# A token-shift stage in one block with three groups under way, and squares and copies moved to ScalarE

## The chip, the core and the metric

The kernel runs on one core of one Trainium2 chip. The metric is the device time of one execution in microseconds (us). Engines are named as in the profile: PE is TensorE (matmuls, with PEld its weight loads), DVE is VectorE, ACT is ScalarE, POOL is GpSimd, SP issues the DMAs.

## What is computed

The program is a whole network over 32 sequences of 113 tokens (36 image patches and 77 text tokens) with 256 features: attention and experts, a state-space stage, a few more feed-forward stages, and at the end of it a token-shift stage and a product-key expert stage. The change touches the token-shift stage alone, whose reference, cut to what matters, is this (`_layernorm` is the outer norm without gain and bias, `_L3_attn_ref` the stage, and its result is added to the residual `h`):

```python
h = h + _L3_attn_ref(_layernorm(h, axis=-1), ...)
# in _L3_attn_ref, per sequence:
h = _layer_norm(x, ln1_g, ln1_b)
hp = _shift(h)
xk = h * mix_k + hp * (1.0 - mix_k)   # xv, xr alike
k = xk @ w_tk; v = xv @ w_tv; r = jax.nn.sigmoid(xr @ w_tr)
y = _wkv(time_decay, time_first, k, v)   # a scan over the tokens
x = x + r * y
h2 = _layer_norm(x, ln2_g, ln2_b)
ck = h2 * cmix_k + hp2 * (1.0 - cmix_k)   # cr alike, hp2 is h2 shifted
kk = jnp.square(jax.nn.relu(ck @ w_ck))
x = x + jax.nn.sigmoid(cr @ w_cr) * (kk @ w_cv)
```

`w_ck` is 256 x 1024 and `w_cv` 1024 x 256; all is fp32. `_wkv` keeps a running maximum, so that its exponentials don't overflow.

## The kernel before

The residual `h` stays in SBUF with the features on the partitions, as two blocks (DK = 2) of 128. Tokens go in 8 groups (GROUPS) of four sequences, 452 columns each (GT), which fill one PSUM bank. `rwkv` (L2184) first loads the weights in a block of its own, in which POOL clears five buffers (L2250 to L2254) and DVE prepares constants (L2259 to L2265). The weights of the channel part come on a semaphore `late`.

Then `step(front, back_cols)` (L2278) is called for group 0 alone, in a loop over seven pairs (the front of group g + 1 beside the back of group g), and for the back of group 7 alone. Each step is one block: all engines meet at its end, and `st.clear()` zeroes the stage's semaphores before the next.

The front of a group is: the input norm and the first norm (`Norm`, L87: mean on PE L107, centring on DVE L135, square on ACT L119 or L2392, variance on PE L113, Ln and Exp on ACT L124 and L127, scaling on DVE L142); gain and bias on DVE (L2484); for each of k, v and r a shifted copy on ACT (L2402), a mix on DVE (L2491) and eight matmul instructions (L2326); copies of k and v out of PSUM on ACT (L2414, L2417); the scan chain, which alternates DVE (L2505 to L2545) and ACT (Exp L2421, L2423, Ln L2426, Exp L2429, L2431); the sigmoids of r and of the gate on ACT (L2434, L2436, with a load of ACT's table ahead, and a load of the Exp/Ln table behind them at L2439); four DVE operations on both feature blocks (L2549 to L2556), which give `x2`; the second norm and its two mixes.

The back of a group is: the channel gate's eight matmul instructions (L2303), the raw copy of the gate on ACT (L2373) and its sigmoid (L2378), eight hidden blocks of four matmul instructions each (L2294), each with a Relu on ACT into one of two buffers (L2367) and its square on DVE (L2450), 32 matmul instructions of the output (L2314), and on DVE the add of `x2` to the residual (L2466), the product with the gate (L2459) and the last add (L2462).

Nothing is planned by a program: each engine's order is the order in the text of its function, and semaphores that count up to constants order the engines among each other.

Of the kernel before, what the change touches and what calls it, by code (L numbers as in the profile page):

```python
# [16 lines left out]
P = 128  # L17
# [67 lines left out]
class Norm:  # L85
# [2098 lines left out]
def rwkv(nc, h, c, wk, wv, wr, ck, cv, cr, cols):  # L2184

# [16 lines left out]
    with Stage(nc, "rw_late") as sl, Stage(nc, "rw") as st:  # L2202
# [11 lines left out]
        h1 = st.sbuf("h1", [P, DK, GT])  # L2214
        back = st.sbuf("back", [P, 5, DK, GT])
# [13 lines left out]
        x2 = st.sbuf("x2", [P, DK, GT])  # L2229
        relu = st.sbuf("relu", [P, 2, GT])  # L2230
# [4 lines left out]
                 "ev_done", "aa_done", "aap_done", "diff_done", "gate_done", "rg_done", "gd_done", "y_done", "ry_done", "x2_done", "h2_done",  # L2235
                 "c_mm", "relu_done", "sq_done", "cr_mm", "cg_raw", "cg_done", "cv_mm", "sk_done", "x3_done", "res_done")
        s = {x: st.sem(x) for x in names}
        with nc.Block() as block:
# [36 lines left out]
        def both(ap):  # L2275
            return ap.rearrange("p k (b n) -> p k b n", n=N)

        def step(front, back_cols):  # L2278

            with nc.Block(no_gpsimd_drain=True) as block:  # L2280
                @block.sync
                def _(sp):
                    if back_cols is None:
                        sp.wait_ge(late, 48)

                @block.tensor
                def _(pe):
                    def hidden(m):
                        if back_cols is None:
                            return  # L2290
                        if m >= 2:
                            pe.wait_ge(s["relu_done"], m - 1)
                        for k in range(DK):
                            mm = nc.tensor.matmul(ps[C_BANK[m % 2]][:, 0:GT], w_ck[:, k, m * P:(m + 1) * P], mixed[:, 3, k, :],  # L2294
                                                  start=(k == 0), stop=(k == DK - 1))
                        mm.then_inc(s["c_mm"], 1)

                    def channel_gate():
                        if back_cols is None:
                            return  # L2300
                        for m in range(DK):
                            for k in range(DK):
                                mm = nc.tensor.matmul(ps[O_BANK[m]][:, 0:GT], W["cr"][:, k, m * P:(m + 1) * P], mixed[:, 4, k, :],  # L2303
                                                      start=(k == 0), stop=(k == DK - 1))
                            mm.then_inc(s["cr_mm"], 1)

                    def channel_out():
                        if back_cols is None:
                            return
                        pe.wait_ge(s["cg_raw"], DK)  # L2310
                        for j in range(DK):
                            for m in range(HB):
                                pe.wait_ge(s["sq_done"], m + 1)
                                mm = nc.tensor.matmul(ps[O_BANK[j]][:, 0:GT], w_cv[:, m, j * P:(j + 1) * P], act2[:, m, :],  # L2314
                                                      start=(m == 0), stop=(m == HB - 1))
                            mm.then_inc(s["cv_mm"], 1)

                    def project(i, x, done):
                        pe.wait_ge(s["mix_done"], DK * (i + 1))
                        for m in range(DK):  # L2320
                            if i == 1 and m == 1:
                                pe.wait_ge(s["k_done"], 1)
                            if i == 2:
                                pe.wait_ge(*((s["k_done"], 2), (s["v_done"], 1))[m])
                            for k in range(DK):
                                mm = nc.tensor.matmul(ps[T_BANK[i][m]][:, 0:GT], W[x][:, k, m * P:(m + 1) * P],  # L2326
                                                      mixed[:, i, k, :], start=(k == 0), stop=(k == DK - 1))
                            mm.then_inc(done, 1)

                    if front is not None:  # L2330
# [783 lines left out]
```

## Time and profile before

| | us |
|---|---|
| three runs | 6014.45, 6021.89 (median), 6035.73 |
| the profiled execution, its own time | 6037.05 |
| its span | 6035.3 |
| PE, DVE, ACT, POOL busy in the span | 4920.7, 3587.9, 2192.0, 2261.7 |
| from the stage's first matmul to its last add | 621.4 |

A row of a table of stretches gives for each engine the time in which it works and the number of its instructions, then the granted clock of PE as a share of full speed. A row of a timeline gives the start, the time that the merged instructions take together, the engine, line and operation, what it writes and reads, how many there are, and in brackets how long the engine had been idle and who ended that. A matmul of the text on fp32 data is shown as two instructions.

### The profile page before, as it was taken

The numbers are of one execution on the slowest core, as the hardware profiler recorded it, in microseconds if no ns is written. First come the engines' busy times: TensorE is split into PE (matmuls) and PEld (weight loads), VectorE is DVE, ScalarE is ACT, GpSimd is POOL, SyncE is SP. The second block draws the span as 40 slices with busy tenths as digits, with TensorE's granted clock in tenths as the row PEclk, the third lists the DMA queues.
The fourth block names the chain that finished last, engine by engine and source line by source line (L and its number), as shares of the span: only waits on it lengthen the run. The fifth ranks groups of instructions, "written<-read, shape, count | busy, mean of one in ns | idle before, by whom it ended". The sixth has DMA issues, their size and how long they took to land. (4 is left out here: it accounts for less than half of the span.)

```text
span 6035.3 us, 64217 instructions
## 1 busy us (share of the span) xinstructions
PE 4920.7 (82%) x21148; PEld 3219.8 (53%) x21148; DVE 3587.9 (59%) x7080; ACT 2192.0 (36%) x4034; POOL 2261.7 (37%) x1366
## 2 busy tenths in 40 slices
PE   7988699368888878888688767857776999999999
PEld 4555377223333333333244437823335998989998
DVE  3664122269889889898742220055554876867776
ACT  3553011055555545656422232234441222222222
POOL 2442300469999989999700000000001212212211
PEclk8998899589999989899889878978887999999999
DMA  1003133212222222222200006600001000000000
GB/s 66 1 1 108 41 120 99 73 57 71 69 68 69 65 70 69 69 71 69 64 0 5 0 0 237 242 3 0 0 0 74 4 3 4 4 3 4 4 4 4
DMA packets 153762, 289.17 MB, mean 48 GB/s; under 512 B 24373, under 2 KB 135468, under 8 KB 144650
## 3 DMA queue, kind: packets, MB, share of 16 engines
q1 hardware_dynamic: 146426, 267.00, 13.6%
q0 software_dynamic: 6144, 14.04, 0.8%
q10 hardware_dynamic: 912, 4.63, 0.2%
q8 instruction: 147, 2.41, 0.2%
q14 instruction: 133, 1.09, 0.1%
HBM read 254.96 MB, written 33.42 MB: 48 GB/s over the span
## 5 line engine op out<-in xcount | busy, mean ns | idle before, releaser
L1496 PE MATMUL ssm_ps<-ssm_hc,net_ident 128*128 128x452 f32 x2048 | 957.1, 594 | 195.3 <-DVE ssm_hc L1729 111.0
L1659 POOL TENSOR_TENSOR ssm_dBu<-ssm_du,ssm_bc 128x904 f32<-128x904 f32 x512 | 1066.6, 2107 | 14.9 <-DMA ssm_bc<-ssm_rows 12.5
L1585 ACT ACTIVATE ssm_ps<-ssm_step,ssm_decay 128x448 f32<-128x448 f32 x1024 | 649.6, 638 | 665.6 <-DVE ssm_ps L1719 433.8
L1496 PEld LDWEIGHTS ssm_ps<-ssm_hc,net_ident 128*128 128x128 f32 x2048 | 390.4, 203 | 728.9 <-issue 343.1
L2925 POOL TENSOR_TENSOR peer_hot_cols<-peer_hot_cols,peer_codesT 128x512 f32<-128x512 f32 (+1 forms) x240 | 288.5, 1202 | 1159.2 <-DVE peer_hot_cols L2941 1159.2
L1719 DVE TENSOR_TENSOR_SCAN ssm_ps<-ssm_ps,ssm_dBu 128x452 f32<-128x452 f32 x512 | 565.2, 1104 | 128.1 <-ACT ssm_ps L1585 43.8
L1719 DVE TENSOR_TENSOR_SCAN ssm_hs<-ssm_ps,ssm_dBu 128x452 f32<-128x452 f32 x512 | 551.7, 1077 | 62.6 <-ACT ssm_ps L1585 35.8
L1668 POOL TENSOR_TENSOR ssm_hc<-ssm_hs,ssm_bc 128x904 f32<-128x904 f32 x256 | 539.5, 2107 | 74.8 <-DVE ssm_hs L1719 74.6
L2835 PE MATMUL peer_ps<-peer_xn,peer_down 128*128 128x226 f32 x2048 | 451.3, 366 | 24.2 <-issue 17.3
L2938 DVE TENSOR_TENSOR peer_hot_rows<-peer_ramp,peer_codesT 128x1024 f32<-128x1024 f32 (+1 forms) x240 | 284.5, 1186 | 280.0 <-PE peer_ps L2850 249.6
L2850 PEld LDWEIGHTS peer_ps<-peer_hot_cols,peer_hot_rows 128*128 128x128 f32 x3616 | 436.0, 192 | 23.8 <-DVE peer_hot_rows L2938 22.6
L2850 PE MATMUL peer_ps<-peer_hot_cols,peer_hot_rows 128*128 128x64 f32 x3616 | 427.7, 272 | 18.7 <-DVE peer_hot_rows L2938 18.7
L2835 PEld LDWEIGHTS peer_ps<-peer_xn,peer_down 128*128 128x128 f32 x2048 | 381.9, 195 | 30.6 <-issue 25.6
L2877 PE MATMUL peer_ps<-peer_hid,peer_up 128*128 128x226 f32 x2048 | 396.7, 354 | 1.5 <-DVE peer_hid L2957 1.5
L2877 PEld LDWEIGHTS peer_ps<-peer_hid,peer_up 128*128 128x128 f32 x2048 | 387.6, 189 | 6.1 <-issue 1.8
L1729 DVE TENSOR_TENSOR ssm_hc<-ssm_ps,ssm_bc 128x452 f32<-128x452 f32 x512 | 309.0, 603 | 0.0
L2904 ACT ACTIVATE peer_hid<-peer_ps 128x452 f32<-128x452 f32 x256 | 140.3, 548 | 416.4 <-PE peer_ps L2835 416.4
L2897 ACT ACTIVATE peer_weight<-peer_ps 128x512 f32<-128x512 f32 (+1 forms) x240 | 144.5, 610 | 287.1 <-PE peer_ps L2850 287.1
L2622 POOL IOTA peer_ramp<- 128x128 f32 x1 | 0.2, 238 | 632.1 <-ACTq L2611 632.1
L2250 POOL MEMSET rw_back<- 128x4520 f32 x1 | 3.9, 3865 | 598.2 <-POOLq L73 598.2
L1283 POOL DMA_INDIRECT sh_got<-slots_out,moe_from_slot x64 | 64.7, 1011 | 420.6 <-SPq L1274 393.1
L1542 PE MATMUL ssm_ps<-ssm_ln_out,ssm_w_in 128*128 128x452 f32 x256 | 138.7, 673 | 97.0 <-DVE ssm_conv L1738 96.8
(422 smaller groups left out, 8304.1 us busy)
## 6 DMA issues: line engine op xcount, KB each, us to landing
ssm_bc<-ssm_rows SPq DMA_DIRECT2D x256, 452.0 KB, 3.6
ex_w<-in_l_ffn_w SPq DMA_DIRECT2D x66, 1024.0 KB, 9.4
moe_w_gu<-in_moe_gate_up SPq DMA_DIRECT2D x16, 704.0 KB
slots_in<-rt_zeros SPq DMA_DIRECT2D x17, 640.0 KB, 8.5
moe_rows_in<-slots_in SPq DMA_DIRECT2D x16, 512.0 KB
slots_out<-xp_rows_out SPq DMA_DIRECT2D x16, 512.0 KB
moe_w_dn<-in_moe_down SPq DMA_DIRECT2D x16, 384.0 KB
peer_down<-in_peer_down_t SPq DMA_DIRECT2D x1, 4096.0 KB, 16.4
```

Source lines behind the costliest of these rows:

```text
L1496: nc.tensor.matmul(Y_BANK[j][:, 0:GT], c["ident"][:, :], hc[:, q % 2, j, :], start=False, stop=(n == S - 1))\
L1585: nc.scalar.activation(rows(dA(i % 2))[:, :, lo:lo + N - 1], rows(step[hf.d][:, j, :])[:, :, lo:lo + N - 1], ACT.Exp, scale=decay[hf.d][:, ...
L1659: nc.gpsimd.tensor_tensor(dBu[:, q % 2, j:j + 2, :], du[hf.d][:, j:j + 2, :], bc[:, q % RING, 0:1, :].to_broadcast([P, 2, GT]), ALU.mult). ...
L1668: nc.gpsimd.tensor_tensor(hc[:, q % 2, 0:2, :], hs[:, q % 2, :, :], bc[:, q % RING, 1:2, :].to_broadcast([P, 2, GT]), ALU.mult).then_inc(s ...
L1719: nc.vector.tensor_tensor_scan(flow(state, hf.d), flow(dA(i % 2), hf.d), flow(dBu[:, q % 2, j, :], hf.d), 0.0, ALU.mult, ALU.add).then_inc ...
L1729: nc.vector.tensor_tensor(hc[:, q % 2, j, :], HS_BANK[:, 0:GT], bc[:, q % RING, 1, :], ALU.mult)\
L2835: mm = nc.tensor.matmul(ps[1 + i % 3][:, jj * PT:(jj + 1) * PT], down[:, m, i * J + jj, :], xn[:, m, :], start=(m == 0), stop=(m == DK - 1))
L2850: mm = nc.tensor.matmul(ps[4 + ch % HB][:, t * PB * EB:(t + 1) * PB * EB], hot_rows[:, at % HB, t, :], hot_cols[:, at % HB, t, :], start=T ...
L2877: mm = nc.tensor.matmul(ps[5 + m][:, 0:PT], w_up[:, j, m * P:(m + 1) * P], hid[:, j, :], start=(j == 0), stop=(j == EB - 1))
L2897: nc.scalar.activation(weight[:, :, :, t0:t0 + n], ps[4 + ch % HB][:, 0:n * PB * EB].rearrange("p (t b j) -> p j b t", b=PB, j=EB), ACT.Co ...
L2925: nc.gpsimd.tensor_tensor(hot_cols[:, at % HB, 0:n, :], hot_cols[:, at % HB, 0:n, :], codesT[:, 2, t0:t0 + n].unsqueeze(2).to_broadcast([P ...
L2938: nc.vector.tensor_tensor(hot_rows[:, at % HB, 0:n, :], ramp[:, :].unsqueeze(1).to_broadcast([P, n, P]), codesT[:, 0, t0:t0 + n].unsqueeze ...
```

## The change

The stage becomes one block. On PE and ACT ten iterations, on DVE eleven, each hold work of three groups: the norms and projections of group i (`early`), the scan chain and second norm of group i - 1 (`mid`), and the channel part of group i - 2 (`late_`). Every wait counts over all groups. `kp`, `v` and `x` get a second buffer; k, v and r share the banks 2 and 3, and the second norm gets bank 1. The square of the Relu goes from DVE to ACT and is made in place; the copy into `AAp` goes from DVE to ACT; the channel gate's sigmoid reads PSUM directly, without the raw copy. `x2` lives in `d1`. The functions that only got a group index (`squares`, `shifted`, `decays`, `weights`, `mix`, `output`, `sums`, `lags`, `averages`, `differences`, `mixed_rows`) issue the operations of before.

```diff
...
-    def __init__(self, st, mean_ps, var_ps, name="ln", width=GT):
+    def __init__(self, st, mean_ps, var_ps, name="ln", width=GT, square=None, out=None):
...
-        self.square = st.sbuf(f"{name}_square", [P, DK, width])
+        self.square = square or st.sbuf(f"{name}_square", [P, DK, width])
...
-        self.out = st.sbuf(f"{name}_out", [P, DK, width])
+        self.out = out or st.sbuf(f"{name}_out", [P, DK, width])
...
-        norms = [Norm(st, ps[0], ps[0], f"ln{i}") for i in range(3)]
-        T_BANK = ((1, 2), (3, 1), (2, 3))
-        C_BANK, O_BANK = (4, 5), (6, 7)
+        T_BANK, C_BANK, O_BANK = (2, 3), (4, 5), (6, 7)
+        x = st.sbuf("x", [P, 2, DK, GT])
+        norms = [Norm(st, ps[0], ps[0], "ln0", out=x)]
+        norms.append(Norm(st, ps[0], ps[0], "ln1", square=norms[0].square))
+        norms.append(Norm(st, ps[1], ps[1], "ln2"))
...
-        kp = st.sbuf("kp", [P, DK, GB, N + 1])
-        v = st.sbuf("v", [P, DK, GT])
+        kp = st.sbuf("kp", [P, 2, DK, GB, N + 1])
+        v = st.sbuf("v", [P, 2, DK, GT])
...
-        x2 = st.sbuf("x2", [P, DK, GT])
-        relu = st.sbuf("relu", [P, 2, GT])
...
-                nc.gpsimd.memset(kp[:, :, :, :], 0.0)
+                nc.gpsimd.memset(kp[:, :, :, :, :], 0.0)
...
+                def project(g, i, x, done):
+                    pe.wait_ge(s["mix_done"], DK * (3 * g + i + 1))
+                    for m in range(DK):
+                        if i == 0 and g:
+                            pe.wait_ge(s["rg_done"], DK * (g - 1) + m + 1)
+                        elif i:
+                            pe.wait_ge((s["k_done"], s["v_done"])[i - 1], DK * g + m + 1)
...
+                def hidden(g, m):
+                    pe.wait_ge(s["mix2_done"], 2 * DK * g + DK)
+                    if HB * g + m >= 2:
+                        pe.wait_ge(s["relu_done"], HB * g + m - 1)
...
+                def channel_gate(g):
+                    pe.wait_ge(s["mix2_done"], 2 * DK * (g + 1))
+                    if g:
+                        pe.wait_ge(s["sk_done"], DK * g)
...
+                def channel_out(g, j):
+                    pe.wait_ge(s["cg_done"], DK * g + j + 1)
+                    for m in range(HB):
+                        pe.wait_ge(s["sq_done"], HB * g + m + 1)
...
+                for i in range(GROUPS + 2):
+                    early, mid, late_ = i, i - 1, i - 2
+                    if i == 2:
+                        pe.wait_ge(late, 48)
+                    if live(early):
+                        if early:
+                            pe.wait_ge(norms[1].log_ready, early)
+                        norms[0].tensor_mean(nc, pe, c["ones"], lambda k: h[:, k, group_cols(early)])
+                    if live(mid):
+                        project(mid, 2, "wr", s["r_mm"])
+                    if live(late_):
+                        hidden(late_, 0)
+                        hidden(late_, 1)
+                    if live(early):
+                        norms[0].tensor_var(nc, pe, c["ones"], early + 1)
+                    if live(late_):
+                        channel_gate(late_)
+                        hidden(late_, 2)
+                        hidden(late_, 3)
+                    if live(early):
+                        pe.wait_ge(norms[0].ready, early + 1)
+                        norms[1].tensor_mean(nc, pe, c["ones"], lambda k: x[:, early % 2, k, :])
+                    if live(late_):
+                        hidden(late_, 4)
+                        hidden(late_, 5)
+                    if live(early):
+                        norms[1].tensor_var(nc, pe, c["ones"], early + 1)
+                    if live(late_):
+                        hidden(late_, 6)
+                        hidden(late_, 7)
+                        channel_out(late_, 0)
+                    if live(early):
+                        project(early, 0, "wk", s["k_mm"])
+                    if live(mid):
+                        pe.wait_ge(s["x2_done"], mid + 1)
+                        if mid:
+                            pe.wait_ge(norms[2].log_ready, mid)
+                        norms[2].tensor_mean(nc, pe, c["ones"], lambda k: d1[:, k, :])
+                    if live(early):
+                        project(early, 1, "wv", s["v_mm"])
+                    if live(mid):
+                        norms[2].tensor_var(nc, pe, c["ones"], mid + 1)
+                    if live(late_):
+                        channel_out(late_, 1)
...
+                def rectify(g, m):
+                    at = HB * g + m
+                    act.wait_ge(s["c_mm"], at + 1)
+                    if g:
+                        act.wait_ge(s["cv_mm"], DK * g)
+                    nc.scalar.activation(act2[:, m, :], ps[C_BANK[m % 2]][:, 0:GT], ACT.Relu).then_inc(s["relu_done"], 1)
+                def square(g, m):
+                    act.wait_ge(s["relu_done"], HB * g + m + 1)
+                    nc.scalar.activation(act2[:, m, :], act2[:, m, :], ACT.Square).then_inc(s["sq_done"], 1)
+                def channel(g, m):
+                    if live(g):
+                        for n in (m, m + 1):
+                            rectify(g, n)
+                        for n in (m, m + 1):
+                            square(g, n)
...
+                def gates(g):
+
+                    if g:
+                        act.wait_ge(s["gd_done"], g)
+                        act.wait_ge(s["ry_done"], g)
...
+                for i in range(GROUPS + 2):
+                    early, mid, late_ = i, i - 1, i - 2
+                    if live(early):
+                        squares(0, early)
+                    if live(mid):
+                        decays(mid, 0)
+                        decays(mid, 1)
+                    channel(late_, 0)
+                    if live(early):
+                        norms[0].scalar_root(nc, act, c["eps"], early + 1)
+                    if live(mid):
+                        for k in range(DK):
+                            act.wait_ge(s["s_done"], DK * mid + k + 1)
+                            if mid:
+                                act.wait_ge(s["aap_done"], DK * mid)
+                            nc.scalar.activation(aa[:, k, :], s_[:, k, :], ACT.Ln).then_inc(s["ln_done"], 1)
+                    channel(late_, 2)
+                    if live(mid):
+                        weights(mid, 0)
+                    if live(early):
+                        squares(1, early)
+                    if live(mid):
+                        weights(mid, 1)
+                        gates(mid)
+                    if live(late_):
+                        channel_gate(late_)
                     nc.scalar.preload_act_table_set(EXP_LN)
+                    if live(early):
+                        norms[1].scalar_root(nc, act, c["eps"], early + 1)
+                    channel(late_, 4)
+                    if live(mid):
                         for k in range(DK):
+                            act.wait_ge(s["aa_done"], DK * mid + k + 1)
+                            if mid:
+                                act.wait_ge(s["diff_done"], DK * mid)
+                            nc.scalar.activation(AAp[:, k, :, 1:N + 1], rows(aa[:, k, :]), ACT.Copy).then_inc(s["aap_done"], 1)
+                    channel(late_, 6)
+                    if live(early):
+                        shifted(early, 0)
+                        shifted(early, 1)
+                    if live(mid):
+                        squares(2, mid)
+                    if live(early):
+                        shifted(early, 2)
                         for k in range(DK):
+                            act.wait_ge(s["k_mm"], DK * early + k + 1)
+                            if early >= 2:
+                                act.wait_ge(s["dl_done"], DK * (early - 1))
+                            nc.scalar.activation(kp[:, early % 2, k, :, 1:N + 1], rows(ps[T_BANK[k]][:, 0:GT]), ACT.Copy)\
+                                .then_inc(s["k_done"], 1)
+                    if live(mid):
+                        norms[2].scalar_root(nc, act, c["eps"], mid + 1)
+                    if live(early):
                         for k in range(DK):
+                            act.wait_ge(s["v_mm"], DK * early + k + 1)
+                            if early >= 2:
+                                act.wait_ge(s["y_done"], early - 1)
+                            nc.scalar.activation(v[:, early % 2, k, :], ps[T_BANK[k]][:, 0:GT], ACT.Copy).then_inc(s["v_done"], 1)
+                    if live(mid):
+                        shifted_channel(mid, 3)
+                        shifted_channel(mid, 4)
...
+                def exponents(g, k):
+                    dve.wait_ge(s["M_done"], DK * g + k + 1)
+                    if g:
+                        dve.wait_ge(s["x3_done"], g)
+                        dve.wait_ge(norms[2].centred_ready, g)
+                        dve.wait_ge(s["aa_done"], DK * g)
...
+                for i in range(GROUPS + 3):
+                    early, mid, late_ = i, i - 1, i - 2
+                    if live(mid):
+                        maxima(mid, 0)
+                        maxima(mid, 1)
+                    if live(early):
+                        centre(0, early, h[:, :, group_cols(early)])
+                    if live(mid):
+                        exponents(mid, 0)
+                        exponents(mid, 1)
+                    if live(late_ - 1):
+                        output(late_ - 1, 1)
+                    if live(mid):
+                        sums(mid, 0)
+                        sums(mid, 1)
+                    if live(early):
+                        input_scale(early)
+                    if live(mid):
+                        lags(mid, 0)
+                        lags(mid, 1)
+                    if live(early):
+                        dve.wait_ge(norms[0].ready, early + 1)
+                        centre(1, early, x[:, early % 2, :, :])
+                    if live(mid):
+                        averages(mid, 0)
+                        averages(mid, 1)
+                    if live(early):
+                        if early:
+                            dve.wait_ge(s["h1_done"], DK * early)
+                        norms[1].vector_scale(nc, dve, early + 1)
+                        scaled(early, norms[1], h1, G1, B1, s["h1_done"], s["mix_done"], DK * 3 * early)
+                    if live(mid):
+                        differences(mid, 0)
+                        differences(mid, 1)
+                    if live(early):
+                        mix(early, 0)
+                    if live(mid):
+                        mixed_rows(mid)
+                    if live(early):
+                        mix(early, 1)
+                    if live(mid):
+                        dve.wait_ge(s["x2_done"], mid + 1)
+                        cols = group_cols(mid)
+                        nc.vector.tensor_tensor(h[:, :, cols], d1[:, :, :], h[:, :, cols], ALU.add).then_inc(s["x3_done"], 1)
+                        centre(2, mid, d1[:, :, :])
+                    if live(late_):
+                        output(late_, 0)
+                    if live(early):
+                        mix(early, 2)
+                    if live(mid):
+                        if mid:
+                            dve.wait_ge(s["h2_done"], DK * mid)
+                        norms[2].vector_scale(nc, dve, mid + 1)
+                        scaled(mid, norms[2], h2, G2, B2, s["h2_done"], s["mix2_done"], 2 * DK * mid)
+                        mix_channel(mid, 3)
+                        mix_channel(mid, 4)
...
-            st.clear()
-        step(group_cols(0), None)
-        with nc.Fori(0, GROUPS - 1) as g:
-            step(group_cols(g + 1), group_cols(g))
-        step(None, group_cols(GROUPS - 1))
+        st.clear()
         sl.clear()
```

## Rows read from the trace of the kernel before

**Rows 1.** The page's head.
```profile
span 6035.3 us, 64217 instructions
```
**Rows 2.** Stretches: first step, a middle step, the last, all (us, then PE, PEld, DVE, ACT, POOL, PEclk, DMA).
```profile
3925.60:3995.20 69.60, 29.28 (x48) 11.48 (x48) 34.37 (x48) 25.65 (x40) 0.00 (x0) 0.67 0.00 0
...
4214.90:4290.00 75.10, 52.71 (x120) 24.76 (x120) 41.92 (x61) 31.42 (x51) 0.00 (x0) 0.82 0.00 0
...
4515.10:4547.00 31.90, 29.97 (x72) 14.64 (x72) 8.65 (x13) 7.73 (x12) 0.00 (x0) 0.92 0.00 1
3925.60:4547.00 621.40, 422.67 (x960) 197.31 (x960) 336.55 (x488) 253.31 (x409) 0.00 (x0) 0.82 0.00 0
```
**Rows 3.** Timeline of PE in the middle step and the last.
```profile
4215.29 3.38 PE L107 MATMUL rw_ps<-net_h,net_ones 128*128 x4 [14.16 <-PEq L73]
...
4239.07 2.18 PE L2294 MATMUL rw_ps<-rw_mixed,rw_ck 128*128 128x452 f32 x4 [3.07 <-ACT rw_relu L2367]
4241.04 4.54 PE L2326 MATMUL rw_ps<-rw_mixed,rw_wk 128*128 128x452 f32 x8
...
4253.00 12.30 PE L2314 MATMUL rw_ps<-rw_act,rw_cv 128*128 128x452 f32 x32
4268.18 3.19 PE L107 MATMUL rw_ps<-rw_x,net_ones 128*128 128x452 f32 x4 [2.88 <-DVE rw_x L2556]
4273.61 2.59 PE L113 MATMUL rw_ps<-rw_ln_square,net_ones 128*128 128x452 f32 x4 [2.25 <-ACT rw_ln_square L119]
...
4520.87 12.30 PE L2294 MATMUL rw_ps<-rw_mixed,rw_ck 128*128 128x452 f32 x32
```
**Rows 4.** Timeline of DVE at the border between two steps.
```profile
4290.18 1.10 DVE L2466 TENSOR_TENSOR net_h<-rw_x,net_h 128x904 f32 x1 [4.88 <-PEq L73]
```
**Rows 5.** Groups of DVE instructions in the stage (busy us, mean ns, idle before).
```profile
L2450 DVE TENSOR_TENSOR rw_act<-rw_relu 128x452 f32<-128x452 f32 x64 | 39.5, 627 | 43.8 <-ACT rw_relu L2367 43.8
...
L2541 DVE COPY rw_AAp<-rw_aa 128x452 f32<-128x452 f32 x14 | 4.7, 380 | 0.0
```
**Rows 6.** Groups of ACT instructions in the stage.
```profile
L2402 ACT ACTIVATE rw_back<-rw_h,rw_rest 128x448 f32<-128x448 f32 x70 | 42.2, 660 | 53.4 <-DVE rw_h L2484 53.4
...
L2367 ACT ACTIVATE rw_relu<-rw_ps 128x452 f32<-128x452 f32 x64 | 34.5, 540 | 45.8 <-PE rw_ps L2294 45.8
...
L119 ACT ACTIVATE rw_ln_square<-rw_ln_centred 128x904 f32<-128x904 f32 x14 | 13.4, 959 | 77.0 <-DVE rw_ln_centred L135 77.0
L124 ACT ACTIVATE rw_ln_log_var<-rw_ps,net_eps 128x452 f32<-128x452 f32 x21 | 13.4, 638 | 47.1 <-PE rw_ps L113 47.1
...
L2436 ACT ACTIVATE rw_gate<-rw_s,rw_first_neg 128x452 f32<-128x452 f32 x14 | 8.7, 673 | 0.0
...
L2423 ACT ACTIVATE rw_d<-rw_d 128x452 f32<-128x452 f32 x14 | 8.1, 582 | 0.2
```
**Rows 7.** Timeline: a hand-off from DVE to ACT, and a table load on ACT.
```profile
4218.83 1.10 DVE L135 TENSOR_TENSOR rw_ln_centred<-net_h,rw_ps 128x904 f32<-128x904 f32 x1 [2.62 <-PE rw_ps L107]
...
4219.96 0.96 ACT L119 ACTIVATE rw_ln_square<-rw_ln_centred 128x904 f32<-128x904 f32 x1 [3.73 <-DVE rw_ln_centred L135]
...
4259.39 1.28 ACT L2434 ACT_TABLE_LOAD   x1
4260.69 0.99 ACT L2434 ACTIVATE rw_rg<-rw_ps 128x452 f32<-128x452 f32 x2
```
**Rows 8.** Timeline of PE in the first step.
```profile
3925.67 3.35 PE L107 MATMUL rw_ps<-net_h,net_ones 128*128 128x452 f32 x4 [14.63 <-PEq L73]
...
3948.99 5.58 PE L2326 MATMUL rw_ps<-rw_mixed,rw_wk 128*128 128x452 f32 x8 [5.55 <-DVE rw_mixed L2491]
...
3957.43 2.82 PE L2326 MATMUL rw_ps<-rw_mixed,rw_wr 128*128 128x452 f32 x7
```
**Rows 9.** Timeline of the setup, POOL and DVE.
```profile
3916.71 0.86 POOL L2251 MEMSET rw_kp<- 128x912 f32 x1
...
3920.04 0.82 DVE L2263 TENSOR_SCALAR rw_drift<-rw_drift,rw_cols 128x452 f32<-128x452 f32 x2 [0.83 <-POOL rw_drift L2254]
```

More of the change, by code:

```diff
@@ L2273, in rows, with flat @@
             return ap.rearrange("p (b n) -> p b n", n=N)
[L2275 to L2292, printed above, removed]
+        def flat(ap):
+            return ap.rearrange("p b n -> p (b n)")
@@ new lines, in live, with _, mean @@
+        def live(g):
+            return 0 <= g < GROUPS
+        with nc.Block(no_gpsimd_drain=True) as block:
+            @block.tensor
+            def _(pe):
+                def mean(j, g, ap):
+                    norms[j].tensor_mean(nc, pe, c["ones"], ap)
+                def project(g, i, x, done):
[5 more added lines that the diff above has]
+                            pe.wait_ge((s["k_done"], s["v_done"])[i - 1], DK * g + m + 1)
@@ L2293, in hidden @@
                         for k in range(DK):
-                            mm = nc.tensor.matmul(ps[C_BANK[m % 2]][:, 0:GT], w_ck[:, k, m * P:(m + 1) * P], mixed[:, 3, k, :],
+                            mm = nc.tensor.matmul(ps[T_BANK[m]][:, 0:GT], W[x][:, k, m * P:(m + 1) * P], mixed[:, i, k, :],
                                                   start=(k == 0), stop=(k == DK - 1))
[L2296 to L2328, printed above, removed]
@@ new lines, in channel_gate @@
+                def channel_gate(g):
+                    pe.wait_ge(s["mix2_done"], 2 * DK * (g + 1))
+                    if g:
+                        pe.wait_ge(s["sk_done"], DK * g)
+                    for m in range(DK):
+                        for k in range(DK):
+                            mm = nc.tensor.matmul(ps[O_BANK[m]][:, 0:GT], W["cr"][:, k, m * P:(m + 1) * P], mixed[:, 4, k, :],
+                                                  start=(k == 0), stop=(k == DK - 1))
+                        mm.then_inc(s["cr_mm"], 1)
@@ new lines, in _, with squares, shifted @@
+            @block.scalar
+            def _(act):
+                def rectify(g, m):
[13 more added lines that the diff above has]
+                            square(g, n)
+                def squares(j, g):
+                    act.wait_ge(norms[j].centred_ready, g + 1)
+                    if j == 0 and g:
+                        act.wait_ge(norms[1].var_ready, g)
+                    nc.scalar.activation(norms[j].square[:, :, :], norms[j].centred[:, :, :], ACT.Square)\
+                        .then_inc(norms[j].square_ready, 1)
+                def shifted(g, i):
+                    act.wait_ge(s["h1_done"], DK * (g + 1))
@@ L2432, in _, with decays @@
-                    for k in range(DK):
-                        act.wait_ge(s["r_mm"], k + 1)
-                        nc.scalar.activation(rg[:, k, :], ps[T_BANK[2][k]][:, 0:GT], ACT.Sigmoid).then_inc(s["rg_done"], 1)
+                        nc.scalar.activation(rows(back[:, i, k, :])[:, :, 1:N], rows(h2[:, k, :])[:, :, 0:N - 1],
+                                             ACT.Copy, scale=rest[:, MIXES[i], k:k + 1]).then_inc(s["back2_done"], 1)
+                def decays(g, k):
+                    act.wait_ge(s["d1_done"], DK * g + k + 1)
+                    nc.scalar.activation(d1[:, k, :], d1[:, k, :], ACT.Exp).then_inc(s["a_done"], 1)
+                    act.wait_ge(s["d2_done"], DK * g + k + 1)
+                    nc.scalar.activation(d2[:, k, :], d2[:, k, :], ACT.Exp).then_inc(s["a_done"], 1)
```

338 lines of the change are left out of this document (131 added, 207 removed).

## The prediction

> **What bounds the kernel now.** I read the page first: 6035.3 us of span, and a program in stages, so what counts is the stage that the diff touches [rows 1]. The table of stretches comes second, with its borders laid on the first and last instruction of the stage's steps [rows 2]. Between the setup and the last residual add lie 621.4 us: a first step of 69.6 us, seven steps of 72 to 75 us (the row of 75.1 stands for them), and a last one of 31.9 us. In a step of 75.1 us PE is busy 52.7 us, DVE 41.9, ACT 31.4. No engine is full: the step is a chain through all three, with PE the longest.
>
> PE's own need comes from two rows of 32 matmuls in 12.30 us [rows 3]: about 0.378 us each, at a granted clock of full speed, for 120 matmuls 45.4 us a group. The other 7.3 us of PE's 52.7 are the half clock: after a wait of 14.16 us four matmuls take 3.38 us instead of about 1.7, and after one of 3.07 us eight take 4.54 instead of 3.2. The step's granted clock is 0.82. The rest of the step, 75.1 less 52.7, is PE waiting.
>
> The timeline of one step says where [rows 4]. The next step's first vector instruction begins at 4290.18 after 4.88 us without work: in this time all engines stand at the block's end and start. Before that PE is idle from 4276.2 on, 14 us with the border, since the second norm, its shift and its mixes run on DVE and ACT alone. PE's two other stops are 3.07 us (a Relu on ACT) and 2.9 plus 2.25 us (the second norm) [rows 3].
>
> **The change, part by part.** (1) Nine blocks become one. The borders go: eight of some 4.9 us, 39 us, and nothing takes their place, since nothing has to be zeroed between groups. (2) In one iteration PE now gets matmuls of three groups, so the norms and mixes of one are covered by the channel matmuls of another. The price is the depth: ten iterations on PE and ACT for eight groups, where there were nine steps. (3) The square of the Relu and the AAp copy go from DVE to ACT. DVE loses 8 x 0.627 and 2 x 0.38 [rows 5], 5.8 us a group, and goes from 41.9 to 36.1. ACT has no row of a 452-wide Square; Exp of that width, 0.58, bounds it from above, and the 904-wide Square (0.96) less half the 904 columns' time from below, about 0.49 [rows 6]. Eight of them, overlapping like the other ACT instructions, add 4 to 5 us. With the copies of AAp in, and the raw copies of the gate out, ACT has some 35 us a group. Neither engine is the bound of an iteration that PE needs 45.4 us for; they count where PE waits on them.
>
> So I walk the new order around once, in the rows' durations. A hand-off costs 0.03 us between DVE and ACT (centred ends at 4219.93, its square begins at 4219.96) [rows 7], and about 0.2 us behind PE's last matmul. Instructions of one engine that don't depend on each other overlap by 0.09 us or so. PE stops at two places of an iteration.
>
> First stop, the hidden product 6, which waits for the Relu 4. That Relu stands in ACT's order behind the first norm's second half. From the end of mean 1: 0.2 + centre 1.13 + square 0.87 + two Exp 0.96 + table load 1.30 + two gates 1.14 + four sigmoids 1.80 + table load 1.30 + log 0.67 + exp 0.48 + Relu 0.58 = 10.4 us. PE covers 12 matmuls of it (4.5 us) and waits 5.9.
>
> Second stop, the v projection, which needs the bank that the copy of k empties, and that copy stands on ACT behind the square of the second norm and a shift. From the end of mean 2: 0.2 + centre 1.13 + square 0.87 + two shifts 1.14 + copy 0.58 = 3.9 us, all of it wait.
>
> The circle closes through PE: the other 108 matmuls are 40.8 us, and 40.8 + 10.4 + 3.9 = **55.2 us** at full clock. To this comes the half clock. Today a step's stops cost 7.3 us of it, 1.3 to 2.4 us for each [rows 2, 3]. Two stops of 5.9 and 3.9 us I set at 2 us each: **59.3 us**. Bounds: nothing, 55.2; or both stops' following eight matmuls at half speed and one more stretch, 66.
>
> What is ahead and behind this: iteration 0 has one group only and the same instructions as today's first step, from its first matmul at 3925.67 to the last projection's place at 3957.43 [rows 8]: 31.8 us. Iteration 1 has 48 matmuls (18.1 us) and waits of 2.6 (input norm) and 3.0 us (first norm), as today's 2 to 3, of 8.1 before the k projection (today's 5.55 of the first step [rows 8] and the two table loads now ahead of the root), and of 4 us (the copy of k). Its clock I take from the first step, 0.67 [rows 2]: two thirds of the matmuls at half speed, 12 us. That is 48. Iterations 2 to 7 are 6 x 59.3 = 356, plus 6 us in the first of them, where the channel products wait for mixes that were late in iteration 1. Iteration 8 has 88 matmuls (33.3) and two waits. Before the hidden product 6: 0.2 + Relu 0.45 + two squares 0.96 + four Exp 1.92 + load 1.30 + gates and sigmoids 2.94 + load 1.30 + Relu 0.58 = 9.65, less the 3.0 of the products 4 and 5, 6.6; before the second norm's variance today's 2.3 [rows 3]; with 1 us of clock 43. The last has 72 (27.2), the same chain without Exps and gates (5.7 less 3.0 = 2.7), 1.6 of clock and 1.3 of output: 33. Sum: 31.8 + 48 + 362 + 43 + 33 = **518 us** for what are 621.4 now: 103 less. Some 44 of the 518 are half clock (4.1 in each of six iterations, 2 in the first, 12 and the rest in the fill and the end). The setup grows by one memset of 0.86 us on POOL ahead of the one that DVE already waits 0.83 us for [rows 9]: 0.8 back. The gain is 102.6 us.
>
> Edits at nothing: the double buffers (no instruction more), the in-place square (it waits for a Relu of its own queue, and a second Relu stands between), the x3 add that now stands behind x2 (covered by PE's work on another group), more waits on the same semaphores. The unrolled order has no jump: the straight first and last steps run at the loop's pace (12.30 us for 32 matmuls in both) [rows 3].
>
> Two rules speak against this. Today's trace shows a load of ACT's table of 1.28 us, and the next ACTIVATE begins 0.02 us behind it [rows 7]. The Trainium skill (ScalarE: Activation LUTs, What ACT_TABLE_LOAD costs) adds a drain of about 1.38 us to each switch. By it the first stop would be 2.8 us longer in each of eight iterations, 22 us in all; the trace has no such time. A square on DVE is 0.627 us here, and a Relu of the same width on ACT 0.54 [rows 5, 6], so the move costs ACT no more than it saves DVE. The Trainium skill (same page, Rules for kernel authors) would keep relu and mul on VectorE; for fp32 of this width the rows don't bear that out.
>
> **Rivals.** (A) The clock stays full: with waits of 9.8 us an iteration in place of 22.4 PE never falls. Then iteration 55.2, the fill without its half-clock parts, 474 us in all, a gain of 147: 5875. For it: between the stops PE has 20 us and more of matmuls without a wait. Against: a wait of 3.07 us brought the half clock today. 0.12.
> (B) The half clock takes more: 64 us an iteration and 10 more in fill and end, 556 in all, a gain of 65: 5957. For it: two stops, 20 us apart, and more of the small ones. 0.10.
> (C) Slower: PE falls to half clock and stays there. 960 matmuls at 0.756 us are 726 us, with some 50 us of waits at fill and end 776, 155 more than now: 6177. It decides from the point where the half clock costs 44 + 103 = 147 us in all, 40% of PE's 363; today it costs 7.3 of 45.4, 16%. For it: PE stops twice in every iteration. Against: it came back after every stop today, even that of 14 us. 0.03. The Trainium skill (TensorE: Matmul & The Clock Gate) tells in its part on HAM oscillation of a kernel whose gaps put it back to the half clock in every tile; by that rule both stops of each iteration would be paid, which the forecast does and no more.
> (D) No change: one queue now holds three groups, and a late one holds up the other two. If that costs 0.3 us at each of some 40 hand-offs, it is 12 us an iteration and 96 in eight: about 6015. Against: the same hand-offs at 0.03 us today. 0.03.
> (E) Each table switch costs its own 1.28 us a second time, as a pause behind it: 2.6 us an iteration, 21 in eight, 5940. Against: the 0.02 us of today [rows 7]. 0.02. It is the case nearest to the drain that the Trainium skill names above.
>
> **How the numbers follow.** The profiled execution took 6037.05 us, 1.75 outside its span, 15 above the median of 6021.89 and above the highest of the three. The stage is fixed work, so I take its difference off the median: 6021.9 - 102.6 = 5919. The profile of the changed kernel should have some 5934 by itself. My forecast has 0.70, and its own range is 5890 to 5950. With A and B in, the range is 5880 to 5960. About 0.3% (18 us) is what a measurement of this kernel can tell from no change. Faster by more: forecast, A, B and E, 0.94; within: D, 0.03; slower: C, 0.03.
>
> **What would show it.** The stage from its first matmul to the last residual add takes about 518 us; from one mean of the input norm to the next 59 us; PE's stops are two an iteration, at the hidden product 6 (released by a Relu) and the v projection (released by the copy of k), of about 6 and 4 us; no 14-us gap; granted clock near 0.9; ACT's load followed at once by a sigmoid; the squares on ACT at 0.5 to 0.58 us. I am wrong if another wait stands in every iteration (the shifts ahead of the first mix, the root of the second norm), if the iteration is over 64 us, or if the clock of the middle iterations is below 0.8.

## The result and the profile after

The changed kernel takes 5939.71 us in the median of four runs (5934.16 to 5946.72), the kernel before 6025.34: 85.6 us less, ratio 0.986 with a 95% interval of 0.984 to 0.988. The range 5880 to 5960 holds it; the 5919 forecast was 21 us too low. Runs of one kernel differ by up to 21 us, so I compare the stage in the profiles, from its first matmul to its last add: 621.0 us before (the borders of the 621.4 in the table of before lie 0.4 us wider), 525.2 after, 95.8 less, which is nearly all of what the spans differ by (96.6).

The table of stretches of the kernel after (columns as in [rows 2]): first iteration, second, third, a middle one, the stage.

```profile
3926.40:3959.80 33.40, 20.93 (x33) 8.38 (x34) 11.24 (x14) 12.01 (x17) 0.00 (x0) 0.61 0.00 0
3959.80:4002.70 42.90, 25.35 (x50) 10.90 (x49) 27.93 (x38) 20.74 (x34) 0.00 (x0) 0.72 0.00 0
4002.70:4065.90 63.20, 50.28 (x122) 23.91 (x121) 39.38 (x55) 37.30 (x67) 0.00 (x0) 0.92 0.00 0
...
4188.90:4250.30 61.40, 51.46 (x122) 24.92 (x121) 36.92 (x52) 33.08 (x59) 0.00 (x0) 0.89 0.00 0
...
3926.40:4451.60 525.20, 419.50 (x960) 199.72 (x960) 295.96 (x408) 271.13 (x476) 0.00 (x0) 0.87 0.00 0
```

An iteration takes 61.4 us where a step took 75.1. PE is busy 51.5 of them, against 52.7: its busy time hardly got less, its waits fell from 22.4 to 9.9 us. The timeline of PE in the middle iteration has them at two places:

```profile
4188.85 1.68 PE L107 MATMUL rw_ps<-net_h,net_ones 128*128 128x452 f32 x4
...
4208.56 1.68 PE L113 MATMUL rw_ps<-rw_ln_square,net_ones 128*128 128x452 f32 x4
4216.29 6.06 PE L2295 MATMUL rw_ps<-rw_mixed,rw_ck 128*128 128x452 f32 x8 [6.05 <-ACT rw_act L2369]
4222.19 6.23 PE L2313 MATMUL rw_ps<-rw_act,rw_cv 128*128 128x452 f32 x16
4228.25 3.20 PE L2286 MATMUL rw_ps<-rw_mixed,rw_wk 128*128 128x452 f32 x8
4231.29 1.68 PE L107 MATMUL rw_ps<-rw_d,net_ones 128*128 128x452 f32 x4
4236.85 6.02 PE L2286 MATMUL rw_ps<-rw_mixed,rw_wv 128*128 128x452 f32 x8 [3.89 <-ACT rw_kp L2482]
```

Both are where the walk put them and as long (6.05 and 3.89; forecast 5.9 and 3.9), and behind each, eight matmuls take 6.06 and 6.02 us instead of 3.20. That answers to [rows 3]; the 14.16 us gap there is gone. In the third iteration the same two stops cost less, as the timeline of PE shows:

```profile
4033.89 5.11 PE L2295 MATMUL rw_ps<-rw_mixed,rw_ck 128*128 128x452 f32 x8 [6.38 <-ACT rw_act L2369]
...
4053.50 4.96 PE L2286 MATMUL rw_ps<-rw_mixed,rw_wv 128*128 128x452 f32 x8 [3.89 <-ACT rw_kp L2482]
```

The timeline of ACT between the two halves of the first norm shows what stands ahead of the Relu 4 (4215.62):

```profile
4206.96 0.96 ACT L2386 ACTIVATE rw_ln_square<-rw_ln_centred 128x904 f32<-128x904 f32 x1 [0.33 <-DVE rw_ln_centred L135]
...
4208.88 1.28 ACT L2420 ACT_TABLE_LOAD   x1
4210.17 1.23 ACT L2420 ACTIVATE rw_gate<-rw_s,rw_first_neg 128x452 f32<-128x452 f32 x2
4211.31 0.96 ACT L2424 ACTIVATE rw_rg<-rw_ps 128x452 f32<-128x452 f32 x2
4212.17 0.98 ACT L2431 ACTIVATE rw_cg<-rw_ps 128x452 f32<-128x452 f32 x2
4213.17 1.28 ACT L2460 ACT_TABLE_LOAD   x1
4214.46 0.64 ACT L124 ACTIVATE rw_ln_log_var<-rw_ps,net_eps 128x452 f32<-128x452 f32 x1
4215.13 0.58 ACT L127 ACTIVATE rw_ln_rstd<-rw_ln_log_var 128x452 f32<-128x452 f32 x1
4215.62 0.97 ACT L2369 ACTIVATE rw_act<-rw_ps 128x452 f32<-128x452 f32 x2
```

As in [rows 7], 0.01 to 0.02 us lie between a load and what follows.

The moved work, by groups of instructions of the stage (busy, mean ns, idle before):

```profile
L2373 ACT ACTIVATE rw_act<-rw_act 128x452 f32<-128x452 f32 x64 | 33.4, 574 | 0.0
...
L2469 ACT ACTIVATE rw_AAp<-rw_aa 128x452 f32<-128x452 f32 x16 | 8.4, 574 | 0.0
```

### The profile page after: what moved, and what is told of

Read it like the earlier page. It is cut to its first block and busy times, and to the rows that moved or that the text cites. A ratio compares the mean times of both kernels' runs of the same rounds, so it can differ in the third digit from the quotient of the medians.

```text
span 5938.7 us, 63636 instructions
## 1 busy us (share of the span) xinstructions
PE 4916.0 (83%) x21148; PEld 3223.0 (54%) x21148; DVE 3547.3 (60%) x7000; ACT 2208.3 (37%) x4101; POOL 2262.6 (38%) x1366
## 5 line engine op out<-in xcount | busy, mean ns | idle before, releaser
L2954 PEld LDWEIGHTS peer_ps<-peer_hot_cols,peer_hot_rows 128*128 128x128 f32 x3616 | 435.7, 192 | 23.6 <-DVE peer_hot_rows L3042 22.4
```

What stands on the lines that cost most here:

```text
L2954: mm = nc.tensor.matmul(ps[4 + ch % HB][:, t * PB * EB:(t + 1) * PB * EB], hot_rows[:, at % HB, t, :], hot_cols[:, at % HB, t, :], start=T ...
```

## The experiments

They ran on three chips, on each of which the kernel before is faster than above. Its median there is 5974.39 us for the runs with one or both stops taken away and the first of the two with extra matmuls, 5967.07 for those on the tables, on the squares and copies with both stops left, and on borders alone, and 5969.57 for the remaining four, among them the changed kernel again:

> The changed kernel itself, beside the reordered one, on the chip of the experiments: stage 525 us, the whole 84 to 96 us under the kernel before, and 70 to 80 us over the run with both reorderings.

Measured: stage 522.9 us, iteration 61.4; 5878.12 us, ratio to the kernel before 0.984 (0.982 to 0.986), 91 us less, and 82 over the run with both reorderings, on another chip. The first iteration took 31.5 us where it took 33.4 in the profile above, the rest agrees within 0.3 us each. I take stages of different runs as comparable within some 3 us; each is from one profile.

**The first stop.**

```diff
                         weights(mid, 1)
+                    channel(late_, 4)
+                    if live(mid):
                         gates(mid)
...
-                    channel(late_, 4)
```

> Relu 4 and 5 of the channel part and their squares go on ScalarE ahead of the gates and the table loads. Theory (two chains set the iteration: PE stops 6.05 us at the hidden product 6 behind ScalarE's table loads, and 3.89 us at the v projection behind the square of the second norm, and each stop costs some 3 us of half clock more): the first stop goes, the second stays at 3.9, the iteration falls from 61.4 to 53 to 56 us, the stage from 525 to 485 to 500 us. Rival (ScalarE's order only hides another wait of the same length, the root of the first norm or the first mix): the iteration stays within 2 us of 61.4.

Measured: stage 488.0 us, iterations 55.8 to 57.5, 5840.27 us. The first stop is gone; small ones of 1.29 (channel gate), 0.46, 0.66 and 1.11 us come up, and the second is 4.06. The rival is out. Behind that second stop, of the same length in every iteration, eight matmuls take between 4.68 and 6.35 us; the timeline of PE has the longest:

```profile
4152.19 6.35 PE L2286 MATMUL rw_ps<-rw_mixed,rw_wv 128*128 128x452 f32 x8 [4.06 <-ACT rw_kp L2483]
```

**The second stop.** The copies of k go up on ACT, ahead of `squares(2, mid)`.

```diff
                         shifted(early, 1)
+                        for k in range(DK):
+                            act.wait_ge(s["k_mm"], DK * early + k + 1)
...
                     if live(mid):
                         squares(2, mid)
```

> The two copies of k out of PSUM go on ScalarE ahead of the square of the second norm and of the shift for r. Theory (two stops): the stop of 3.89 us at the v projection goes with its half clock, the first stop stays at 6 us, the iteration falls from 61.4 to 52 to 56 us, the stage from 525 to 480 to 500 us. Rival (the wait moves on to the variance of the second norm, which now comes later): the iteration stays within 2 us of 61.4.

Measured: stage 479.0 us, iteration 54.6, 1 us under what was expected, the first stop unchanged at 6.04, 5833.46 us. The iteration fell by 6.8 us, of which the wait is 3.9 and the half clock behind it 2.8 (6.02 less 3.20). The timeline of PE at the first stop:

```profile
4124.30 6.13 PE L2295 MATMUL rw_ps<-rw_mixed,rw_ck 128*128 128x452 f32 x8 [6.04 <-ACT rw_act L2369]
```

**Both.** The two edits together.

> Both reorderings at once. Theory: no stop of PE over 3 us is left in the middle iterations, the granted clock there is 0.97 or more, the iteration is 49 to 53 us (PE needs 45.4), the stage 445 to 470 us, the whole 55 to 80 us below the changed kernel, some 5870 us. Rival (vector work and hand-offs form a chain of their own of nearly the same length): the iteration does not fall below 57 us.

Measured: 5795.68 us, ratio to the kernel before 0.971 (0.968 to 0.973), stage 447.8, iteration 50.1. The stretch of a middle iteration, and behind it the timeline of PE in a later one:

```profile
4040.40:4090.50 50.10, 46.57 (x121) 22.47 (x120) 36.79 (x52) 33.05 (x59) 0.00 (x0) 1.00 0.00 0
```

The timeline:

```profile
4111.76 3.20 PE L2295 MATMUL rw_ps<-rw_mixed,rw_ck 128*128 128x452 f32 x8
4116.24 4.82 PE L2313 MATMUL rw_ps<-rw_act,rw_cv 128*128 128x452 f32 x12 [1.29 <-ACT rw_cg L2431]
4121.52 1.78 PE L2313 MATMUL rw_ps<-rw_act,rw_cv 128*128 128x452 f32 x4 [0.46 <-ACT rw_act L2373]
4123.97 3.30 PE L2286 MATMUL rw_ps<-rw_mixed,rw_wk 128*128 128x452 f32 x8 [0.66 <-DVE rw_mixed L2528]
4128.38 1.78 PE L107 MATMUL rw_ps<-rw_d,net_ones 128*128 128x452 f32 x4 [1.11 <-DVE rw_d L2619]
```

The granted clock is 1.00 and 3.5 us of waits are left. PE is busy 46.6 of the 50.1 us and DVE 36.8, so vector work is not the bound. This beats both kernels: 75 us of stage less than the changed one (522.9), 82 us in the medians, which come from two chips (87 us when each is taken against the kernel before on its own chip).

**The clock alone.** The stops stay, and PE gets work in them that nobody reads, in a bank that is free there. One matmul of the text is two instructions of the timeline.

```diff
+                def idle_work(bank, count, sem, at):
+                    pe.wait_ge(sem, at)
+                    for _ in range(count):
+                        nc.tensor.matmul(ps[bank][:, GT:512], c["ones"][:, :], c["ones"][:, 0:512 - GT], start=True, stop=True)
...
+                        idle_work(1, 16, norms[2].log_ready, mid)
                         hidden(late_, 6)
...
+                        idle_work(0, 10, norms[1].log_ready, early + 1)
```

> At each of the two stops PE gets matmuls of 60 columns on the constant matrix, whose result nobody reads (16 ahead of the hidden product 6, 10 ahead of the v projection, in banks that are free there). Nothing else changes. Theory (the difference between 61.4 and 55.2 us is the half clock behind the two stops): the granted clock of the middle iterations rises from 0.89 to 0.97 or more and the iteration falls to 55 to 57 us, the stage to 485 to 500 us. Rival (the clock only accompanies the stops, and another wait would take its place): the iteration stays within 2 us of 61.4, or rises by what the matmuls take.

Measured: iteration 57.6 to 58.8, stage 505.1, granted clock 0.94 to 0.97: iteration and stage above what was expected, since the extra matmuls took 3.68 and 2.34 us and left 2.53 and 1.72 us open. Behind the second stop eight matmuls took 3.27 us, behind the first still 4.96 to 6.12. A second run with more of them (26 and 16):

> As the run with extra matmuls at the stops, but 26 and 16 of them, so that they fill more of the 6.05 and 3.89 us (16 and 10 left 2.53 and 1.72 us open, and the clock was lost for half the time behind the first). Theory (what lies between 58.4 and 55.2 us is the half clock still left behind the first stop): granted clock 0.99 or 1, iteration 55 to 56 us, stage 480 to 492 us. Rival (the extra matmuls delay the ones behind them as much as they save): iteration 58 us or more.

Its timeline of PE at the two stops:

```profile
4135.25 5.91 PE L2293 MATMUL rw_ps<-net_ones 128*128 128x60 f32 x52
4141.45 3.27 PE L2300 MATMUL rw_ps<-rw_mixed,rw_ck 128*128 128x452 f32 x8 [0.29 <-ACT rw_act L2377]
...
4155.18 3.68 PE L2293 MATMUL rw_ps<-net_ones 128*128 128x60 f32 x32
4159.23 3.27 PE L2286 MATMUL rw_ps<-rw_mixed,rw_wv 128*128 128x452 f32 x8 [0.37 <-ACT rw_kp L2490]
```

Measured (timeline above): iteration 55.9 us, stage 492.0, clock 1.00, 5850.75 us. From the start of the four matmuls ahead of a stop to the start of those behind it as much time passes as before (7.72 and 5.57 us, against 7.73 and 5.56), so 5.5 of the 61.4 us are the half clock and nothing else, and the 55.2 us of the walk at full clock are met within 0.7.

**The table switches.** `ACT.Sigmoid` becomes `ACT.Relu` at three places, and the `preload_act_table_set(EXP_LN)` of each iteration goes. This kernel leaves the sigmoid function out and computes something else; it serves for its times alone (one run).

> The three sigmoids are made as Relu, so that ScalarE never loads another table in the stage; the sigmoid function is left out, the rest is computed on those values. Theory (the chain to the Relu 4 sets the first stop): the first stop shortens by twice 1.3 us to some 3.4 us, the iteration falls by 2.6 to 5 us to 56 to 59 us, the stage by 20 to 40 us. If a pause stood behind each switch, it would fall by 5 us and more for that alone. Rival (the table loads are covered): iteration 61.4 within 1 us.

PE's timeline at the first stop, in two iterations in turn:

```profile
4134.10 3.27 PE L2295 MATMUL rw_ps<-rw_mixed,rw_ck 128*128 128x452 f32 x8 [3.19 <-ACT rw_act L2369]
...
4188.85 4.97 PE L2295 MATMUL rw_ps<-rw_mixed,rw_ck 128*128 128x452 f32 x8 [3.20 <-ACT rw_act L2369]
```

Measured: the first stop shrinks by 2.86 us to 3.19, the iteration to 54.8, stage 483.2. The wait falls by the two loads (2 x 1.28 and the 0.02 behind each) and 0.3 us, so no pause of a load's length stands behind a switch here. The Trainium skill (ScalarE: Activation LUTs, What ACT_TABLE_LOAD costs) has a drain of about 1.38 us for each; the measurement decides. The iteration falls by 6.6, more than expected, since the half clock behind this stop went as well (3.27 us for eight) and the second's eight took 4.97. That holds for four of the five iterations with this stop. In the fifth the same stop cost 1.8 us (4.97 for eight), the second's eight took 6.12, and the iteration 57.6.

**Which engine squares and copies.** The squares back on DVE in pairs (a `square(late_, m)` behind the sums, the lags, the first norm's scaling and the differences):

> The eight squares of the Relu go back to VectorE, in the new order, two each behind the sums, the lags, the scaling of the first norm and the differences. Theory (the squares lie in the cover of PE's work on either engine): iteration 61.4 within 1 us, stage 525 within 5 us. Rival (moving the squares to ScalarE carries part of the gain, since VectorE's chain gets 5 us shorter): the iteration grows by 2 to 5 us, the stage by 15 to 40 us.

Measured: iteration 61.4 us, stage 519.7, DVE busy 41.4 us an iteration instead of 36.9, ACT 29.3 instead of 33.1. The stage is 5.5 us under the profile above and 3.2 under the changed kernel's second one, where within 5 of the first was expected. The rival, 15 to 40 us more, is out: the move brought nothing. The AAp copy back on DVE:

> The copy into AAp goes back to VectorE, right behind the averages. Theory (VectorE waits 5 us there for the root of the first norm, and the copy fits in): iteration 61.4 within 0.5 us, stage 525 within 3 us. Rival (ScalarE's copies stand ahead of the Relus 6 and 7, and taking them away shortens PE's stop): the iteration falls by 1 to 2 us.

Measured, in one run: iteration 61.4, stage 525.0. The same. And with both stops gone, the squares on DVE (the third pair then stands behind the averages):

> Both reorderings, and the eight squares of the Relu on VectorE. Theory (with the two stops gone ScalarE's queue ahead of the channel gate sets a stop of 1.3 us, and two squares less ahead of it take it away, while VectorE gets 5 us more ahead of the first mix): iteration 49 to 52 us, stage 440 to 455 us, within 1% of the run with both reorderings. Rival (once PE is nearly full VectorE's chain is the bound, so the squares belong on ScalarE): iteration 54 us and more, stage over 470 us.

Measured: iteration 50.0, stage 446.2, ratio 0.972 (0.970 to 0.974) beside 0.971 for the other engine. PE then waits 0.35 us for the channel gate instead of 1.29, and 1.97 for a square.

**The borders.** A block for each iteration, without zeroing:

```diff
-        with nc.Block(no_gpsimd_drain=True) as block:
+        for it in range(GROUPS + 3):
+            with nc.Block(no_gpsimd_drain=True) as block:
```

> Each iteration becomes a block of its own again, with all engines meeting at its end; nothing is zeroed, and the order inside is the changed kernel's. Theory (the borders were worth some 5 us each and PE's wait on top): ten inner borders add 5 to 9 us each, the iteration is 67 to 71 us, the stage 575 to 615 us, so most of the gain is gone. Rival (the gain is from three groups on each engine, and borders fall into PE's stops): the stage grows by less than 25 us.

Measured: stage 530.6 us, iterations 59.3 to 62.2, PE's pause at a border mostly 1.1 us, DVE's 0.49. Timelines of PE and DVE at one border:

```profile
4197.39 1.76 PE L107 MATMUL rw_ps<-net_h,net_ones 128*128 128x452 f32 x4 [1.09 <-PEq L2273]
...
4197.49 2.11 DVE L2557 TENSOR_TENSOR_SCAN rw_Mp<-rw_kp,rw_drift 128x456 f32<-128x456 f32 x2 [0.49 <-PEq L2273]
```

Here the theory fell: borders alone cost 5 to 8 us in all, not 50 to 90, and the second iteration alone, 51.2 us for 42.9, grew by as much. In the middle ones the pause is made up for by less half clock (PE busy 49.4 to 49.9 us, where it was 51.5). So I added the zeroing (a further stage of 63 semaphores, its `clear()` behind each block):

> As the run with a block for each iteration, and behind each a second block that zeroes 63 semaphores of its own which nothing else uses, as many as the kernel before zeroed behind each step. Theory (the meeting of the engines costs about 1 us, and the zeroing the rest of the 4.9 us of the kernel before): VectorE's pause at the border is 4.5 to 5.3 us, PE's 5 us and more, the iteration 65 to 69 us, the stage 575 to 610 us. Rival (the 4.9 us came from the loop's jump and its registers, not from the zeroing): the pause stays under 2.5 us and the stage under 555 us.

The timeline of PE at a border of this run:

```profile
4235.18 3.12 PE L107 MATMUL rw_ps<-net_h,net_ones 128*128 128x452 f32 x4 [5.14 <-PEq L73]
```

And that of DVE at the same border:

```profile
4235.29 2.11 DVE L2559 TENSOR_TENSOR_SCAN rw_Mp<-rw_kp,rw_drift 128x456 f32<-128x456 f32 x2 [4.54 <-PEq L73]
```

Measured: stage 595.9 us, iteration about 68.2, the pauses in the middle 5.1 to 5.8 us (PE) and 4.5 to 5.2 (DVE), 5941.22 us. So nearly all of the pause of [rows 4] is the zeroing in a block of its own; there is no loop here, so it is not the jump. Ten of them cost 65 us, 6.5 each: 4 or a little more of wait, the rest half clock behind it (PE busy 52.6 us an iteration instead of 49.9).

## Why the prediction was right, point by point

- **The walk.** Circle at full clock 55.2 us: shown, by 55.9 with the clock kept. Both stops at their place and length: shown by taking each away.
- **The term that was mis-sized** is "Two stops of 5.9 and 3.9 us I set at 2 us each". The half clock takes 2.9 and 2.8 us (6.06 and 6.02 less 3.20). With 61.4 for 59.3 that is 11 us in the fourth to the eighth iteration; the second and third gave 7 of them back, the first, ninth and last were 4 over, and the stage is 7 over, within rounding. I had taken 2 us from the 1.3 to 2.4 of the kernel before, where no stop showed more than 2.5, and had put the rest into rival B. The 1.3 was itself short: behind the wait of 3.07 us of [rows 3] four matmuls took 2.18 us instead of 1.68 before the eight that took 4.54, so it cost 1.8.
- **Fill and end.** 33.4 and 42.9 us for the first two iterations (31.8 and 48), 63.2 for the third (65.3), 44.9 for the ninth (43), 33.6 for the last (33). The second was 5 under, since its half clock took 7 us (PE busy 25.4 for 18.1 of work), not 12; its clock was 0.72, not 0.67. The third was 2 under: the late mixes brought some 3 us of waits and not 6, and its two stops cost 1.9 and 1.8 us of half clock, near the 2 each of the forecast.
- **The sum**: 525.2 against 518, 7 of the 21 us that the forecast was low. The other 14 are no fault of the walk: the fourth run of the kernel before put its median 3.5 us up, and the medians fell by 10 us less than the stage. For the profiled execution I had named 5934; it took 5940.44, 6 more. The profiled spans fell by 96.6 us, the medians by 85.6, and on the chip where it was run again by 91; runs of the kernel before spread by 21 us here and by up to 25 there, so where those 10 us went stays open.
- **Part 1, the borders**, was sized at 39 us by the DVE pause of 4.9. In the new order ten borders with zeroing cost 595.9 less 525.2, 71 us; without zeroing 5. So, counted in this order, 65 of the 96 us hang on not zeroing between groups, which the single block allows, and few on the engines' meeting. I had put down both as one, and without the half clock behind each.
- **Part 2, three groups**: with borders like those of before in place it is worth 621.0 less 595.9, 25 us, though with ten borders for eight. The forecast's split, 39 us for the borders and some 64 for the rest, was wrong; its total did not hang on it, since it came from the walk. How much three groups would bring in the old order without zeroing was not run.
- **Part 3, squares and copies on ACT**: said to touch no bound, and it does not. A square took 0.574 us on ACT, at the top of the bracket 0.49 to 0.58. DVE went to 36.9 us an iteration (forecast 36.1), ACT to 33.1 (some 35).
- **Setup**: the stage's first matmul starts 0.76 us later (forecast 0.8).
- **Rivals.** A is out: the clock fell at both stops. B's 64 us an iteration was nearer than it looked, 2.6 us off where the forecast was 2.1 off, and its 5957 lies 17 us from the measured median, the forecast's 5919 21: the stage (525, against 518 and 556) speaks for the forecast, the median alone would not. C is out: the clock of the middle iterations is 0.89. D is out: DVE's centre ends at 4206.93 and ACT's square begins at 4206.96, 0.03 us as before. E's 5940 is the measured time, by chance: no load has a pause behind it, and taking both loads away shortened the stop by 2.9 us, not by 5.1.

## What to carry to other kernels

Walk a software pipeline's order once around with the durations of the trace before it is built: it gives the period and names the stops, and here two moves of a few lines in ScalarE's queue, a Relu ahead of a table switch and a bank's copy ahead of a square that waits, were worth 75 us, nearly as much as the whole rewrite. Price a stop of PE at its wait plus the half clock behind it, here anything from 0.1 to some 3 us. Ask of a border what it is made of: the meeting was cheap here, the zeroing of semaphores in a block of its own was not.

## What the runs showed of the hardware

- In the steady iterations of the changed kernel a stop of 6.05 and one of 3.89 us cost nearly the same half clock (2.9 and 2.8 us). In its third iteration the stop of 3.89 us cost 1.8. In the run without switches a stop of 3.19 us cost 0.1 us four times (3.27 us for the eight matmuls behind it) and one of 3.20 us 1.8 (4.97). So the length of the wait alone does not give the price, even at one place of one kernel.
- Matmuls of 60 columns kept the clock at 1.00 through both stops (52 instructions in 5.91 us, 32 in 3.68), with 0.29 and 0.37 us left open.
- In the middle iterations a meeting of the engines at a block's end took 0.49 us on DVE and 1.1 to 1.4 on PE, against 4.5 to 5.2 on DVE and 5.1 to 5.8 on PE with a block behind it that zeroes 63 semaphores.
